# Two job clusters per segment, output projections one segment later, softmax sums on VectorE alone

## What is computed

```python
x = x + tanh(g_xattn) * attention(layernorm(x), ctx)      # q from x; k, v from ctx
x = x + tanh(g_ffn) * ffn(layernorm(x))

attn = clip(q @ k.T / 8, -11, 11); attn = softmax(attn)   # per head, 2048 x 1601
out = (attn @ v, heads side by side) @ Wo + bo

w = w quantised to 4 bits in blocks of 32                 # gate, up, down
act_qdq(a) = round(a / s) * s, s = max|a| / 32767         # over the whole tensor
```

## Time and profile before

| | us |
|---|---|
| median of 3 runs | 1286.16 (1285.85 to 1286.87) |
| the profiled execution, its own time | 1289.14 |
| its span in the trace | 1287.2 |
| TensorE busy in the span | 1137.3 |
| VectorE busy | 1114.6 |
| GpSimd busy | 735.1 |
| ScalarE busy | 599.4 |

### The profile page before, as it was taken

The page is one execution under the profiler, slowest core; times in us unless marked ns, Lnnn a source line. Parts: engine busy times, 40 slices in busy tenths (PEclk is TensorE's granted clock), DMA queues, the critical chain, the costliest instruction groups (busy, mean ns, idle before and its releaser), DMA issues.

```text
span 1287.2 us, 21518 instructions
## 1 busy us (share of the span) xinstructions
PE 1137.3 (88%) x8427; PEld 497.1 (39%) x8427; DVE 1114.6 (87%) x1435; ACT 599.4 (47%) x682; POOL 735.1 (57%) x457
## 2 busy tenths in 40 slices
PE   4999999999999999999999999998789987699028
PEld 2443333333333333333333333333223332487028
DVE  7588988898889888988898889899899999848986
ACT  2454444444444444444444444443345443249542
POOL 1596666666666666666666666667676565102400
PEclk9999999999999999999999999999899999699559
DMA  4000000000000000000000020000000000000002
GB/s 153 1 2 13 6 1 1 17 2 1 1 18 1 1 1 17 1 1 1 18 1 1 1 69 23 2 1 1 1 1 1 2 1 1 1 1 1 0 1 66
DMA packets 17108, 13.90 MB, mean 11 GB/s; under 512 B 2222, under 2 KB 16751, under 8 KB 17007
## 3 DMA queue, kind: packets, MB, share of 16 engines
q1 hardware_dynamic: 17006, 12.53, 3.1%
HBM read 10.43 MB, written 2.10 MB: 10 GB/s over the span
## 4 chain that ended last, share of the span: by engine, by line
PE 48%; DVE 34%; issue 11%; ACT 6%; POOL 1%; DMA 0%; POOLq 0%; SPq 0%; DVEq 0%
PE ps L938 14%; DVE e_buf L667 13%; PE ps L922 13%; PE ps L1033 6%; DVE rden L635 5%; DVE oT L643 4%; DVE acc L628 4%; PE ps L860 3%; PE ps L869 3%; PE ps L852 3%; PE ps L895 3%; ACT e_buf L446 2%; PE ps L880 1%; DVE xacc L658 1%; ACT z L501 1%
## 5 line engine op out<-in xcount | busy, mean ns | idle before, releaser
L347 POOL TENSOR_TENSOR acc<-acc,e_buf 128x512 f32<-128x512 f32 (+1 forms) x352 | 574.2, 1631 | 289.3 <-DVE e_buf L667 284.7
L446 ACT ACTIVATE e_buf<-ps 128x1024 f32<-128x1024 f32 x416 | 426.2, 1025 | 475.0 <-PE ps L922 467.6
L667 DVE TENSOR_SCALAR e_buf<-e_buf 128x1024 f32<-128x1024 f32 x416 | 475.1, 1142 | 116.7 <-ACT e_buf L446 114.3
L938 PE MATMUL ps<-e_buf,vb 64*64 64x512 f32 x3328 | 444.6, 605 | 61.1 <-DVE e_buf L667 44.8
L628 DVE TENSOR_TENSOR acc<-acc,e_buf 128x512 f32<-128x512 f32 (+1 forms) x352 | 259.8, 738 | 0.0
L938 PEld LDWEIGHTS ps<-e_buf,vb 64*64 64x64 f32 x3328 | 113.1, 133 | 294.7 <-issue 166.3
L922 PE MATMUL ps<-qb,kb_even 64*64 64x512 f32 x1664 | 216.9, 592 | 1.3 <-ACT e_buf L446 1.3
L922 PE MATMUL ps<-qb,kb_odd 64*64 64x512 f32 x1664 | 217.7, 593 | 0.0
L347 POOL TENSOR_TENSOR acc<-e_buf 128x512 f32<-128x512 f32 x32 | 81.8, 2556 | 70.3 <-DVE e_buf L667 70.3
L922 PEld LDWEIGHTS ps<-qb,kb_odd 64*64 64x64 f32 x1664 | 64.2, 134 | 116.0 <-issue 111.8
L635 DVE RECIPROCAL rden<-ps 128x128 f32<-128x128 f32 x124 | 109.0, 919 | 0.0
(11 more groups left out here) (105 smaller groups left out, 754.4 us busy)
## 6 DMA issues: line engine op xcount, KB each, us to landing
xacc<-in_x_dram SPq DMA_DIRECT2D x4, 512.0 KB, 7.5
wst<-in_L_xattn_Wkv_dram SPq DMA_DIRECT2D x16, 128.0 KB, 2.4
out_dram<-z SPq DMA_DIRECT2D x8, 256.0 KB, 2.1
e_buf<-in_ctx_dram SPq DMA_DIRECT2D x3, 512.0 KB, 4.7
wst<-in_L_xattn_Wq_dram SPq DMA_DIRECT2D x8, 128.0 KB, 2.3
wo_raw<-in_L_xattn_Wo_dram SPq DMA_DIRECT2D x8, 128.0 KB, 3.1
z<-in_L_ffn_w_gate_dram SPq DMA_DIRECT2D x1, 768.0 KB, 4.9
z<-in_L_ffn_w_up_dram SPq DMA_DIRECT2D x1, 768.0 KB, 6.8
```

The lines of the kernel that those rows point to most:

```text
L347: pool.tensor_tensor(acc[0:r, t0 % 2, 1, :], a, e_buf[0:r, (ST * t0 + st) % E_BUFS, 1, :], ALU.add).then_inc(sum_b, 1)
L446: nc.scalar.activation(e_buf[:, g % E_BUFS, :, :], sc[:, g % 2, :, :], ACT.Exp, scale=float(DH) ** -0.5).then_inc(exp_done, 1)
L667: dve.tensor_scalar(tile, tile, EXP_LO, EXP_HI, ALU.max, ALU.min).then_inc(clip_done, 1)
L938: ins = pe.matmul(ps_o[DH * h:DH * h + DH, half, :], vb[rows, p % 2, st, DH * h:DH * h + DH], e_buf[rows, g % E_BUFS, h, :], start=(st == ...
```

## The change

- In an ordinary segment the jobs stand in two clusters: k, v and q at st 0, and at st 6 the two y halves of the segment before the last (t - 2 in place of t - 1), followed by den of the last segment. Segments 28 to 30 keep their jobs, and 28 has both the y of segment 26 (at st 6) and the y of segment 27 (at st 10).
- VectorE adds both heads in one instruction of 128x1024 (`add_e`), with one semaphore. GpSimd's sums go away.
- `e_buf` has 6 buffers in place of 4.
- On VectorE, up to segment 27, `add_y` stands at st 8 (of segment t - 2), `invert` at 9 and 10, `scale_out` at 11. From segment 28 on they stay at 12, 6, 7 and 8, and the last piece of `w_low` moves from 9 to 8.
- On ScalarE `q_take` stands at st 2 behind k and v.
- The weight pieces are prepared one in every second segment from 14 to 24, at st 3 to 6, with the two multiplications on VectorE. SyncE loads them in segment 4.
- The bias is added by VectorE in four instructions of 128x1024, at st 4 to 7 of segment 0.

```diff
-WQ0, WT0 = SEGS - 7, SEGS - NBS
-E_BUFS = 4
+WQ0, WT0 = SEGS // 2 - 2, SEGS - NBS
+E_BUFS = 6
...
     if p < PAIRS:
-        jobs = [(0, ("k", p, t % NBS)), (0, ("v", p, t % NBS)), (4, ("q", t + 1)), (4, ("den", t - 1))]
-    else:
-        jobs = [(0, ("wT", wm, 0)), (0, ("wT", wm, 1)), (4, ("q", t + 1)), (4, ("den", t - 1)), (6, ("wT", wm, 2))]
+        jobs = [(0, ("k", p, t % NBS)), (0, ("v", p, t % NBS)), (0, ("q", t + 1))]
+        if t >= 2:
+            jobs += [(6, ("y", t - 2, 0)), (6, ("y", t - 2, 1))]
+        return jobs + [(6, ("den", t - 1))]
+    jobs = [(0, ("wT", wm, 0)), (0, ("wT", wm, 1)), (4, ("q", t + 1)), (4, ("den", t - 1)), (6, ("wT", wm, 2))]
+    if t == WT0:
+        jobs += [(6, ("y", t - 2, 0)), (6, ("y", t - 2, 1))]
     return jobs + [(10, ("y", t - 1, 0)), (10, ("y", t - 1, 1))]
...
             def run(seg):
+                if seg.t0 == NBS:
+                    load_ffn_weights()
...
-                for st in range(1, ST):
-                    r = rows_of(st)
...
-                    pool.tensor_tensor(acc[0:r, t0 % 2, 1, :], a, e_buf[0:r, (ST * t0 + st) % E_BUFS, 1, :],
-                                       ALU.add).then_inc(sum_b, 1)
...
-                        act.wait_ge(sum_a, back.count(ST - 1, s0))
-                        act.wait_ge(sum_b, back.count(ST - 1, s0))
+                        act.wait_ge(summed, back.count(ST - 1, s0))
...
-                    if st == 6 and t0 + 1 < SEGS:
+                    if st == (2 if p < PAIRS else 6) and t0 + 1 < SEGS:
                         q_take(seg, t0 + 1)
...
+            def add_e(seg, st):
...
-                dve.tensor_tensor(acc[0:r, t0 % 2, 0, :], a, e_buf[0:r, (ST * t0 + st) % E_BUFS, 0, :],
-                                  ALU.add).then_inc(sum_a, 1)
+                dve.tensor_tensor(acc[0:r, t0 % 2, :, :], a, e_buf[0:r, (ST * t0 + st) % E_BUFS, :, :],
+                                  ALU.add).then_inc(summed, 1)
...
+                    if t0 == 0 and 4 <= st < 4 + NBS:
+                        add_bias(st - 4)
                     last = t0 == SEGS - 1
...
+                    if st == 8 and 2 <= t0 <= WT0:
+                        add_y(seg, t0 - 2, 0)
+                        add_y(seg, t0 - 2, 1)
                     for c in ((), range(4))[t0 >= 1]:
-                        if st == (4 if last else 6) + c // 2:
+                        if st == (4 if last else 6 if t0 >= WT0 else 9) + c // 2:
                             invert(seg, t0 - 1, c)
-                    if st == (6 if last else 8) and t0 >= 1:
+                    if st == (6 if last else 8 if t0 >= WT0 else 11) and t0 >= 1:
                         scale_out(seg, t0 - 1)
...
-                    if st == (9 if last else 12) and t0 >= 1:
+                    if WQ0 <= t0 < WQ0 + 12 and (t0 - WQ0) % 2 == 0:
+                        w = (t0 - WQ0) // 2
+                        if st == 3:
+                            w_scales(w)
+                        if st == 4:
+                            w_multiply(w, 2, w_inverse, w_scaled)
+                        if st == 5:
+                            w_integers(w)
+                        if st == 6:
+                            w_multiply(w, 1, w_round, w_quant)
+                    if st == (9 if last else 12) and t0 >= WT0:
                         add_y(seg, t0 - 1, 0)
                         add_y(seg, t0 - 1, 1)
...
-                pe.wait_ge(sum_a, s.count(ST - 1, ST - 1))
-                pe.wait_ge(sum_b, s.count(ST - 1, ST - 1))
+                pe.wait_ge(summed, s.count(ST - 1, ST - 1))
```

More of the change, by code:

```diff
@@ L279, in _, with load_ffn_weights @@
             load_pair(1, 1)
+            def load_ffn_weights():
+                await_taken(sp, ("lT", NBS - 1, 1))
+                for n, w in enumerate((w_gate, w_up)):
+                    sp.dma_start(zf[:, n * FT * DM:(n + 1) * FT * DM].rearrange("p (t d) -> p t d", d=DM),
+                                 w.rearrange("(t p) d -> p t d", p=P)).then_inc(in_w, 16)
+                for n in range(KT):
+                    sp.dma_start(wpiece[4 + n], w_down[P * n:P * n + P, :]).then_inc(in_w, 16)
             def run(seg):
+                if seg.t0 == NBS:
+                    load_ffn_weights()
                 if seg.t0 % NBS != NBS - 1 or (seg.t0 + 5) // NBS >= PAIRS:
@@ L290, in _ @@
             segments(sp, run)
[L292 to L297, removed]
             for g in range(NT // 2):
@@ L617, in w_low, with w_multiply, add_bias @@
                                   ALU.subtract).then_inc(job_taken[bank_of(key)], 1)
-            def add_a(seg, st):
+            def w_multiply(w, row, ready, done):
+                blocks = wpiece[w].rearrange("p (n e) -> p n e", e=QB)
+                dve.wait_ge(ready, w + 1)
+                dve.tensor_tensor(blocks, blocks, wsc[:, w, row, :].unsqueeze(2).to_broadcast([P, WBLK, QB]),
+                                  ALU.mult).then_inc(done, 1)
+            def add_e(seg, st):
                 t0, r = seg.t0, rows_of(st)
                 if st == 1:
-                    a = e_buf[:, (ST * t0) % E_BUFS, 0, :]
+                    a = e_buf[:, (ST * t0) % E_BUFS, :, :]
                 else:
-                    a = acc[0:r, t0 % 2, 0, :]
-                    dve.wait_ge(sum_a, seg.count(ST - 1, st - 1))
+                    a = acc[0:r, t0 % 2, :, :]
+                    dve.wait_ge(summed, seg.count(ST - 1, st - 1))
                 dve.wait_ge(clip_done, seg.count(ST, st + 1))
-                dve.tensor_tensor(acc[0:r, t0 % 2, 0, :], a, e_buf[0:r, (ST * t0 + st) % E_BUFS, 0, :],
-                                  ALU.add).then_inc(sum_a, 1)
+                dve.tensor_tensor(acc[0:r, t0 % 2, :, :], a, e_buf[0:r, (ST * t0 + st) % E_BUFS, :, :],
+                                  ALU.add).then_inc(summed, 1)
+            def add_bias(b):
+                dve.wait_ge(bias_scaled, 1)
+                dve.wait_ge(lat_pool, NT - 4)
+                rows = xacc[:, 4 * b:4 * b + 4, :]
+                dve.tensor_tensor(rows, rows, bo_t[:, :].unsqueeze(1).to_broadcast([P, 4, DM]), ALU.add).then_inc(bias_added, 1)
             def invert(seg, t, c):
@@ L668, in run @@
                     if st >= 2:
[L669 removed]
+                        add_e(seg, st - 1)
                     elif st == 0 and t0 >= 1:
[L671 to L672 removed]
+                        add_e(Seg(t0 - 1), ST - 1)
+                    elif t0 >= 1:
                         join_out(seg, t0 - 1)
+                    if t0 == 0 and 4 <= st < 4 + NBS:
+                        add_bias(st - 4)
                     last = t0 == SEGS - 1
+                    if WT0 <= t0 < WT0 + 3:
+                        for j in {3: (0, 1), 8: (2,)}.get(st, ()):
+                            w_low(t0 - WT0, j)
+                    if st == 8 and 2 <= t0 <= WT0:
+                        add_y(seg, t0 - 2, 0)
+                        add_y(seg, t0 - 2, 1)
                     for c in ((), range(4))[t0 >= 1]:
[L676 removed]
+                        if st == (4 if last else 6 if t0 >= WT0 else 9) + c // 2:
                             invert(seg, t0 - 1, c)
[L678 removed]
+                    if st == (6 if last else 8 if t0 >= WT0 else 11) and t0 >= 1:
                         scale_out(seg, t0 - 1)
[L680 to L688, removed]
[L689 removed]
+                    if WQ0 <= t0 < WQ0 + 12 and (t0 - WQ0) % 2 == 0:
[9 more added lines that the diff above has]
+                    if st == (9 if last else 12) and t0 >= WT0:
                         add_y(seg, t0 - 1, 0)
```

10 lines of the change are left out of this document (5 added, 5 removed).

## The result

The changed kernel takes 1388.4 us (median of 4 runs, 1385.5 to 1391.5) against 1286.5: slower, ratio 1.079, 95% interval 1.076 to 1.082. The profiled execution took 1385.52 us with a span of 1383.7, which is 96.5 us more span than before. 1383 us had been forecast, in a range of 1335 to 1410.

The account below looks back on a forecast made before the run. TensorE was taken as the bound, VectorE nearly level. To the profiled 1289.1 us came +78 (segments: (a), (c), (d)), +13 (e) and +6 (f), making 1386; less 3.0, 1383 us, range 1335 to 1410.

Parts of the forecast that it names:

- (a): One job cluster less: the dearer first values group goes once, -0.16 us a segment, -4 us for 26 segments.
- (b): Sums on VectorE: clip always 0.60 us, sum 1.14; a step costs 1.74 us against TensorE's 1.72.
- (c): Cluster at st 6: den waits about 1.6 us for its bank, until VectorE has added y half 0.
- (d): Segment's end: reciprocals and scaling delay clips; segments take 35.6 or 33.0 us, +78 us with (a) and (c).
- (e): Weight preparation: -20 us from the old place, +21 for unhidden pieces, +12 for lowered clock: +13 us.
- (f): Segments 0, 1 and 28 to 31: waits in 28, fuller VectorE in 30 and 31, bias: together +6 us.
- (g): Six buffers, SyncE's load in segment 4 and q_take at st 2: put at nothing.
- R1: TensorE stays the bound, VectorE ahead at den and tiles 10 to 12, weights hidden: 1231 us; chance 0.09.
- R2: Only (d) holds, den's wait is hidden because y is taken in time: 1335 us; chance 0.14.
- R3: TensorE's clock falls in ordinary segments too, another 2 us in each of 26: 1433 us; chance 0.09.

Follow-up runs that it names:

- e1: Changed kernel, but VectorE adds the two y halves at step 7, ahead of tile 8's clip, in segments 2 to 27: 1332.2 us, ratio 1.034.
- e2: As e1, and the four reciprocals stand together at VectorE's step 8: 1280.0 us, ratio 0.994.
- e3: Changed kernel, y halves unmoved, reciprocals one at each of steps 9 to 12, output scaling at step 12, up to segment 27: 1359.2 us, ratio 1.055.
- e4: Changed kernel, but the four operations on a weight piece stand together at VectorE's step 2: 1352.1 us, ratio 1.049.
- e8: As e2, and the weight pieces stand at VectorE's step 2: 1258.2 us, ratio 0.976.
- e9: As e8, but in segment 28 segment 26's output projection stands at TensorE's step 8 and is taken at VectorE's step 10: 1254.3 us, ratio 0.973.
- e10: As e9, but output scaling of segments up to 26 moves to VectorE's step 2 of the next segment: 1237.3 us, ratio 0.961.
- e7: Changed kernel with the sums of head 1 back on GpSimd: 1461.8 us, ratio 1.135.
- e5: Changed kernel with 4 exponential buffers in place of 6: 1390.9 us, ratio 1.080.

## Why the prediction was right, point by point

The forecast said +97 us on the profiled execution, and the spans differ by 96.5. The closeness is partly luck. By medians the kernel is 101.9 us slower: the execution profiled before was 3.0 us above its median, the one after 2.9 below, so the forecast of the median misses by 5. And inside the sum, misses of a few us cancel, as (e) and (f) show. The mechanism is the one that was forecast.

**(a), (b).** Right in kind. There are two dearer first groups of values in a segment now and each still takes 1.02 us in the chain; that one less is worth 4 us was not measured by itself. The sum of 1024 columns has a duration of 1.22 and takes 1.13 or 1.14 from start to start (474.09 to 475.22, 472.35 to 473.49); the clip takes 0.54 to 0.61. The prediction says of the Trainium skill ("VectorE: DVE Perf Modes", The DRAIN you can't avoid) that the timeline disagrees with it. That is too strong: the same paragraph adds that an operation which is not held starts earlier. The starts, 1.13 apart for durations of 1.22, speak only against taking its first sentence without that addition.

**(c).** Right in kind; den's wait was sized at 1.6 us and is 1.78. The sum for it starts tile 8's clip when its exponential has ended; in the trace the clip starts 0.15 us later (473.49 against 473.34), as VectorE is still at the sum before it. The five steps before it show why: VectorE's clips start 1.74 us apart (464.79 to 473.49), the exponentials 1.72 (463.73 to 472.32), and so a small lateness builds up. That den's wait alone is worth 45 us in 26 segments is shown by the first experiment.

**(d).** Right. A segment was worked out at 35.6 and 33.0 us and takes 35.4 and 33.2; four in a row take 139.5 us against 127.6 before. Over 26 segments that is +78 us, the number forecast. The late clips were put at "some 2 us" and are 1.41 + 0.48 and a small one. The second and third experiments show them apart from (c).

**(e).** Right, with nothing hidden: the intervals with a piece are longer by 6.2, 6.2, 5.2, 6.2, 5.2 and 5.9 us, 34.9 together where 33 were expected, against 20 before: +15 for +13. A piece's work had been put too low, at 3.5 us: in e4 it takes 4.1, as the first multiplication takes 0.99 in place of 0.87 and the rounding 0.60 in place of 0.40 (both start to start; three quarters of the clip's 0.60 would have been 0.45 already). That leaves some 10 us for the clock, where 12 were forecast. The long wait was expected at 4.5 us and is 4.41, with half clock behind it:

```profile
625.23 1.98 PE L882 MATMUL ps<-acc,ones 128*64 128x512 f32 x4 [4.41 <-DVE xacc L652]
```

**(f).** The two waits in segment 28 were worked out at 2.4 and 1.4 us:

```profile
1069.75 1.13 PE L897 MATMUL ps<-wo_g,oT 128*128 128x256 f32 x4 [2.38 <-DVE rden L629]
1072.02 2.07 PE L897 MATMUL ps<-wo_g,oT 128*128 128x256 f32 x4 [1.14 <-DVE wgu L596]
```

The sum of this term, +6, was too high. What the trace leaves for it is 96.5 - 78 - 15 - 3 (two falls of the clock, below) = about 0. In it lies an earlier start: the first query copy in segment 0 comes at 52.98 us in place of 55.70. The change is hardly the reason. In the profiles of all twelve kernels this copy comes either at 53.0 to 53.4 us or at 55.3 to 55.9, and e8 and e9, which do not differ before segment 28, have it at 53.06 and 55.39. So it varies from one execution to another; why was not traced. Without these 2.7 us the term is about +3, half of what was forecast.

**(g).** Four buffers against six was measured: nothing. That ScalarE's and SyncE's moves cost nothing fits the sum, but they were not tried alone.

**The rivals.** R1 did not happen, for the reason that was named: VectorE was too late at den and at tiles 10 to 12, and the last experiment reaches it once both are mended. R2 is the first experiment, at 1332 us where 1335 had been worked out. R3 happened in only two of the changed kernel's 20 segments that have no weight piece; in e7, with GpSimd's sums, it happened in all 26. The prediction calls R3 the result of the Trainium skill's rule ("TensorE: Matmul & The Clock Gate", HAM oscillation). That likeness was loose: the kernel described there idles for longer in each iteration than den does here.

## What to carry to other kernels

Where two engines have nearly equal work, their sums of busy time don't tell which order is faster: here VectorE's busy time fell by 36 us and the kernel became 102 us slower, and two places in VectorE's order gave it all back. For every job that takes a shared bank, ask which instructions stand ahead of the one that frees it, on the other engine's queue. And put work that no one awaits where the engine rests (here behind a cluster of TensorE's jobs), not where it has a deadline at every step.

## What the runs showed of the hardware that was not expected

The same wait of TensorE did not always bring its granted clock down. It fell behind all six waits of 4.41 us in the changed kernel's profile and behind all 26 of 3.96 to 5.50 us in that of e7, as it had behind the 3.10 us of the earlier trace rows. In e1, den waits 2.68 us in the six segments with a weight piece; behind two of these waits den itself took 1.98 us in place of 1.08, and the intervals of these two segments are 2.6 and 1.5 us longer than a piece costs in the other four, where the clock stayed up. One of the two:

```profile
806.44 1.98 PE L882 MATMUL ps<-acc,ones 128*64 128x512 f32 x4 [2.68 <-DVE xacc L652]
```

In the changed kernel the clock also fell behind two of the 20 waits of 1.78 us. Behind the first of them the groups took up to 1.95 us in place of 1.04:

```profile
370.61 1.08 PE L882 MATMUL ps<-acc,ones 128*64 128x512 f32 x4 [1.78 <-DVE xacc L652]
371.62 1.57 PE L940 MATMUL ps<-e_buf,vb 64*64 64x512 f32 x8
372.95 1.95 PE L924 MATMUL ps<-qb,kb_even 64*64 64x512 f32 x8
```

That segment took 36.72 us in place of 35.41, and the one with the other, at 965 us, 37.08. The same wait, in the same place of the loop, thus costs 1.3 to 1.7 us more in two segments. e3, e4 and e5, which keep den's wait, have two or three such long segments each; e1, e2, e8, e9 and e10, where den no longer waits in ordinary segments, have none. The changed kernel's runs spread over 6 us where the kernel before spread over 1.6. The mean granted clock was 0.949 in the two shorter ones (1385.5 and 1386.4 us) and 0.946 in the two longer ones (1390.4 and 1391.5). That fits more such falls in the longer ones, which have no kept trace, so it is likely but not shown. Falls behind the wait of 1.78 us can't be the only reason for such a spread: the executions of e2, whose ordinary segments don't have it, spread over 6.6 us, with the lowest clock (0.950) in the longest.
